# Combination, second gate and quantised feed-forward part in one block by batches, with the last weights quantised beside the first gate and the routing

## What is computed

```
x   = x + y0 * silu(layernorm(x))            # first gate, y0 from the first scan
xn  = layernorm(x); p, idx = top4(softmax(xn @ router))
x   = x + shared_expert(xn) + sum_k p[k] * expert[idx[k]](xn)   # the sum over k: "combination"
x   = x + y1 * silu(layernorm(x))            # second gate, y1 from the second scan
# last feed-forward part, weights in three values, activations in 8 bits, per token
ws  = mean(|W|) + eps;  Wq = clip(round(W / ws), -1, 1)      # for w_gate, w_up, w_down
xs  = 127 / max|xn|;    xq = min(round(xn * xs), 127)
h   = silu(xq @ Wq_gate / ..) * (xq @ Wq_up / ..)            # 2048 columns
hs  = 127 / max|h|;     hq = min(round(h * hs), 127)
out = x + (hq @ Wq_down) / ..
```

## Time and profile before

| | us |
|---|---|
| median of 3 runs (2230.44 to 2234.99) | 2232.67 |
| profiled execution, device time | 2233.23 |
| span of the profiled execution | 2231.4 |
| combine, second gate and last feed-forward part, of the span | 371.6 |

### The profile page before, as it was taken

How to read it: one execution, slowest core, us unless ns; L and a number is a source line. 1 busy time by engine, 2 the same in 40 slices (tenths; PEclk the granted TensorE clock), 3 DMA queues, 4 the chain that set the end, 5 groups by cost and what they waited for, 6 DMA issues and landing times. The chain is left out here.

```text
span 2231.4 us, 27149 instructions
## 1 busy us (share of the span) xinstructions
PE 1653.2 (74%) x8480; PEld 954.2 (43%) x8502; DVE 1758.9 (79%) x2275; ACT 1143.2 (51%) x1765; POOL 1337.3 (60%) x648
## 2 busy tenths in 40 slices
PE   5666757656538548999799998999989991005998
PEld 1222213222217435676466654666556660003554
DVE  3999999999965836998589867888578885856886
ACT  4675766766633014443444445555455550734776
POOL 0779788779953003888088844888368884652111
PEclk7888888989976569999999998999989996557999
DMA  6346546447552820000000432444424227650000
GB/s 218 117 162 202 183 154 231 145 158 248 179 196 76 160 68 11 10 10 15 33 11 1 149 135 97 157 166 156 161 102 156 86 72 289 190 159 2 23 25 29
DMA packets 127144, 264.63 MB, mean 119 GB/s; under 512 B 44546, under 2 KB 48386, under 8 KB 121794
## 3 DMA queue, kind: packets, MB, share of 16 engines
q1 hardware_dynamic: 93890, 184.24, 24.7%
q0 software_dynamic: 11520, 37.76, 5.8%
q10 hardware_dynamic: 21600, 40.90, 4.9%
HBM read 180.41 MB, written 82.44 MB: 118 GB/s over the span
## 5 line engine op out<-in xcount | busy, mean ns | idle before, releaser
L470 POOL TENSOR_TENSOR ssm_hs<-ssm_hs,ssm_Cs 128x1024 f32<-128x1024 f32 x128 | 314.7, 2458 | 146.5 <-DVE ssm_hs L433 142.5
L470 POOL TENSOR_TENSOR moe_hs<-moe_hs,moe_Cs 128x1024 f32<-128x1024 f32 x128 | 301.4, 2355 | 98.5 <-DVE moe_hs L433 97.5
L433 DVE TENSOR_TENSOR_SCAN moe_hs<-moe_dA,moe_bu 128x1024 f32<-128x1024 f32 x128 | 292.6, 2286 | 20.0 <-ACT moe_dA L347 10.1
L433 DVE TENSOR_TENSOR_SCAN ssm_hs<-ssm_dA,ssm_bu 128x1024 f32<-128x1024 f32 x128 | 292.7, 2287 | 17.3 <-ACT ssm_dA L347 0.5
L460 POOL TENSOR_TENSOR moe_U<-moe_U,moe_hs 128x1024 f32<-128x1024 f32 x128 | 302.0, 2360 | 6.0
L280 PE MATMUL ssm_pY<-ssm_hs,ssm_ident 128*128 128x512 f32 x512 | 276.9, 668 | 2.8 <-POOL ssm_hs L470 2.8
L1195 PE MATMUL moe_pgu<-moe_xsh,all_Wreg 128*128 128x256 f16 x1408 | 255.3, 279 | 12.8 <-DVE moe_hsl L1440 11.3
L1245 PE MATMUL moe_pgu<-all_Wreg,moe_xth 128*128 x1280 | 243.6, 313 | 0.0
L258 PE MATMUL ssm_pB<-ssm_bc,ssm_sel 96*128 96x512 bf16 x128 | 54.7, 427 | 204.9 <-DVE ssm_bu L424 204.6
L1195 PE MATMUL moe_pgu<-moe_xsl,all_Wreg 128*128 128x256 f16 x704 | 196.9, 280 | 0.0
L665 POOL TENSOR_TENSOR ssm_wlo<-ssm_wst,ssm_whi 128x1360 f16<-128x1360 f32 x64 | 186.5, 2914 | 0.0
(11 more groups left out here) (238 smaller groups left out, 3457.7 us busy)
## 6 DMA issues: line engine op xcount, KB each, us to landing
ssm_wst<-in_w_all SPq DMA_DIRECT2D x64, 680.0 KB, 4.9
w_hi<-ssm_whi SPq DMA_DIRECT2D x64, 340.0 KB, 2.3
w_lo<-ssm_wlo SPq DMA_DIRECT2D x64, 340.0 KB, 3.1
y_d<-moe_yo ACTq DMA_DIRECT2D x80, 256.0 KB
all_Wreg<-w_hi SPq DMA_DIRECT2D x16, 1088.0 KB
all_Wreg<-w_lo SPq DMA_DIRECT2D x16, 1088.0 KB
ssm_Cs<-c_d SPq DMA_DIRECT2D x64, 256.0 KB, 5.6
gate_Y<-y_ssm ACTq DMA_DIRECT2D x8, 1024.0 KB, 9.2
```

The lines of the kernel that those rows point to most:

```text
L433: self.nc.vector.tensor_tensor_scan(self.hs[:, j, :, :].rearrange("p k t -> p (k t)"), self.dA[:, q, :, :].rearrange("p k t -> p (k t)"), ...
L470: self.nc.gpsimd.tensor_tensor(self.hs[:, j, :, :], self.hs[:, j, :, :], self.Cs[:, i:i + 1, :].to_broadcast([P, HC, L]), ALU.mult)\
```

## The change

There are two parts.

**Ternary.** A new class holds the quantisation of the weights. In `gate(nc, 0, ...)` the eight pieces of w_gate and w_up are loaded by ACT's queue, and quantised matrix by matrix: ACT takes the absolute sums with an activation (`act_abs`) that DVE took, DVE and PE make the total and the scale, ACT does `up` (`act_up`), **POOL clips** (`pool_clip`, a tensor_scalar of 128x2048 in place, which DVE did), ACT does `out` and issues a store to DRAM. In `routing` the four pieces of w_down go the same way; DVE's total stands at g = 4 and its scale at g = 8 of the 64 steps. The last stage loads the three bfloat16 matrices (2 MB each) again.

**tail.** `combine`, `gate(nc, 1, ...)` and `quant_ffn` become one function with one block. Combination and second gate run ahead of the feed-forward loop by batches: nine tiles (AHEAD) are combined before the loop and one in each of the first seven steps; the four tiles of the next batch are gated after fixed parts of the loop (GATED), with y's transpose going through one PSUM buffer (`py`); the gate activations of the batch after the next are made by ACT in every fourth step, and Y and G have room for two batches. There are 16 gather buffers in place of 8.

```diff
 def gate(nc, l, d, X, y_ssm, r):
...
             def _(act):
...
+                if l == 0:
+                    for j in range(8):
+                        Q.act_load(act, j // 4, j % 4)
...
                     def evac(b):            # per tile c, behind the copy L803
+                        if b == 0:
+                            Q.act_up(act, 0, c)
+                        if b == 1:
+                            Q.act_out(act, 0, c)
+                            Q.act_abs(act, 1, c)
+                            Q.store(act, 0, c)
+                        if b == 2:
+                            Q.act_up(act, 1, c)
+                        if b == 3:
+                            Q.act_out(act, 1, c)
+                            if c:
+                                Q.store(act, 1, c - 1)
...
+                    Q.act_abs(act, 0, 0)
+                    Q.act_abs(act, 0, 1)
                     second(0)
+                    Q.act_abs(act, 0, 2)
                     second(1)
+                    Q.act_abs(act, 0, 3)
...
+                    Q.store(act, 1, 3)
+                    Q.stored(act)
...
             def _(pool):                    # behind the 16 products L820
+                for j in range(8 if l == 0 else 0):
+                    Q.pool_clip(pool, j // 4, j % 4)
...
 # DVE behind layernorm(b), PE ahead of router(b), for b in (0, 2)
+                            Q.dve_total(dve, b // 2)
+                            Q.dve_scale(dve, b // 2)
+                            Q.pe_total(pe, b // 2, ones[:])
...
 def routing(nc, d, r):
...
+                for k in range(4):          # ACT: 4 abs, 4 up, 4 x (out, store)
+                    Q.act_abs(act, 0, k)
...
+            def _(pool):
+                for k in range(4):
+                    Q.pool_clip(pool, 0, k)
...
+    def pool_clip(self, pool, z, k):
+        w = self.W[:, z, k, :]
+        pool.wait_ge(self.up_rdy, 4 * z + k + 1)
+        self.nc.gpsimd.tensor_scalar(w, w, ROUND + 1.0, ROUND - 1.0, ALU.min, ALU.max).then_inc(self.clip_rdy, 1)
...
+def tail(nc, d, r, X, y_ssm, out):          # POOL
+                for i in range(KC + 2):
+                    fetch(i)
+                for i in range(KC):
+                    y_gate(i)
+                fetch(KC + 2)
+                fetch(KC + 3)
+                x_clip(0)
+                for i in range(KC, 2 * KC):
+                    y_gate(i)
+                fetch(2 * KC)
+                for i in range(TT):
+                    if i + AHEAD < TT:
+                        fetch(i + AHEAD)
+                    if i + 1 < TT:
+                        x_clip(i + 1)
+                    b, t = divmod(i, KC)
+                    if t == KC - 1 and b + 2 < B:
+                        for j in range(KC):
+                            y_gate((b + 2) * KC + j)
...
+                for i in range(KC):         # DVE, ahead of its loop
+                    combine(i)
+                norm(0, 0, c_sd, c_rs, c_ln)
+                combine(KC)
+                combine(KC + 1)
+                for i in range(KC):
+                    gated(i)
+                norm(1, 0, a_sd, a_rs, a_ln)
                 x_scale(0)
+                combine(KC + 2)
                 x_scale(1)
+                combine(KC + 3)
+                norm(0, 1, c_sd, c_rs, c_ln)
+                combine(2 * KC)
                 for i in range(TT):
...
+                        if b + 1 < B and (t, f) in GATED:
+                            gated((b + 1) * KC + GATED[t, f])
...
+                    if i + AHEAD < TT:
+                        combine(i + AHEAD)
                     if i:
                         add(i - 1)
...
-        combine(nc, d, r, X, Wq, wsc)
-        gate(nc, 1, d, X, y_ssm, r)
-        quant_ffn(nc, d, r, X, Wq, wsc, out)
+        tail(nc, d, r, X, y_ssm, out)
```

More of the change, by code:

```diff
@@ L50 @@
 SHIFT = 2
+GATED = {(0, 3): 0, (1, 0): 1, (1, 2): 2, (1, 3): 3}
 def shared_pieces(c):
@@ L936, in _ @@
                 nc.scalar.activation(r["sig"][:], r["logit"][:, :, E], ACT.Sigmoid).then_inc(fin, 1)
+                for k in range(4):
+                    Q.act_abs(act, 0, k)
+                for k in range(4):
+                    Q.act_up(act, 0, k)
+                for k in range(4):
+                    Q.act_out(act, 0, k)
+                    Q.store(act, 0, k)
+                Q.stored(act)
+            @block.gpsimd
+            def _(pool):
+                for k in range(4):
+                    Q.pool_clip(pool, 0, k)
             @block.vector
@@ L1657, in quant_ffn @@
         pd = m.ps("pd", [P, H])
+        py = m.ps("py", [P, KC, P])
         loaded = m.sem("loaded")
+        w_in = [m.sem(f"w_in{i}") for i in range(3)]
+        y_in = [m.sem(f"y_in{i}") for i in range(B)]
+        got = [m.sem(f"got{i}") for i in range(NR)]
+        used = m.sem("used")
+        c_st = m.sem("c_st")
+        c_mv = m.sem("c_mv")
+        c_sd = m.sem("c_sd")
+        c_rs = m.sem("c_rs")
+        c_ln = m.sem("c_ln")
+        g_rdy = m.sem("g_rdy")
+        yg_rdy = m.sem("yg_rdy")
+        tr_rdy = m.sem("tr_rdy")
+        xa_rdy = m.sem("xa_rdy")
+        a_st = m.sem("a_st")
+        a_mv = m.sem("a_mv")
+        a_sd = m.sem("a_sd")
+        a_rs = m.sem("a_rs")
+        a_ln = m.sem("a_ln")
         eps_rdy = m.sem("eps_rdy")
-        sd_rdy = m.sem("sd_rdy")
-        ln_rdy = m.sem("ln_rdy")
         step = m.sem("step")
@@ L1692, in _, with fetch, y_gate, x_clip @@
                 sp.wait_ge(o_out, 16 * TT)
+            @block.gpsimd
+            def _(pool):
+                def fetch(i):
+                    for k in range(TOPK):
+                        g = i * TOPK + k
+                        if g >= NR:
+                            pool.wait_ge(used, g - NR + 1)
+                        nc.gpsimd.indirect_dma_start(
+                            out=yr[:, g % NR, :], out_offset=None, in_=r["y_d"],
+                            in_offset=bass.IndirectOffsetOnAxis(ap=r["pos"][:, i, k:k + 1], axis=0)).then_inc(got[g % NR], 16)
+                def y_gate(i):
+                    b, t = divmod(i, KC)
+                    if t == 0:
+                        pool.wait_ge(y_in[b], 16)
+                    pool.wait_ge(g_rdy, i + 1)
+                    y = Y[:, b % 2, t, :]
+                    nc.gpsimd.tensor_tensor(y, y, G[:, b % 2, t, :], ALU.mult).then_inc(yg_rdy, 1)
+                def x_clip(i):
+                    pool.wait_ge(xr_rdy, i + 1)
+                    if i >= 2:
+                        pool.wait_ge(tx_rdy, i - 1)
+                    nc.gpsimd.tensor_scalar(xq[:, i % 2, :], xn[:, i % 2, :], -ROUND, 127.0, ALU.add,
+                                            ALU.min).then_inc(xq_rdy, 1)
+                for i in range(KC + 2):
[13 more added lines that the diff above has]
+                        x_clip(i + 1)
+                    b, t = divmod(i, KC)
+                    if t == KC - 1 and b + 2 < B:
+                        for j in range(KC):
+                            y_gate((b + 2) * KC + j)
             @block.vector
@@ L1784, in _ @@
                 act.wait_ge(rnd_set, 1)
+                act.wait_ge(eps_rdy, 1)
+                root(0, 0, c_mv, c_sd)
+                for i in range(KC):
+                    gate_of(i)
+                root(1, 0, a_mv, a_sd)
                 layernorm(0)
@@ L1788, in _ @@
                 x_evac(0)
+                root(0, 1, c_mv, c_sd)
+                for i in range(KC, 2 * KC):
+                    gate_of(i)
                 for i in range(TT):
+                    b, t = divmod(i, KC)
                     for f in range(FC):
                         g = i * FC + f
+                        if f == 1 and t == 2 and b + 1 < B:
+                            root(1, b + 1, a_mv, a_sd)
+                        if f == 1 and t == 3 and b + 2 < B:
+                            root(0, b + 2, c_mv, c_sd)
                         act.wait_ge(gu_rdy, g + 1)
@@ L1802, in _ @@
                             layernorm(i + 2)
+                        if f >= 2 and t == 3 and b + 2 < B:
+                            for j in range(2):
+                                gate_of((b + 2) * KC + 2 * (f - 2) + j)
                     if i + 1 < TT:
@@ L1810, in _, with y_transpose @@
                     h_evac(TT - 1, a)
-            @block.gpsimd
-            def _(pool):
-                for i in range(TT):
-                    pool.wait_ge(xr_rdy, i + 1)
-                    if i >= 2:
-                        pool.wait_ge(tx_rdy, i - 1)
-                    nc.gpsimd.tensor_scalar(xq[:, i % 2, :], xn[:, i % 2, :], -ROUND, 127.0, ALU.add,
-                                            ALU.min).then_inc(xq_rdy, 1)
             @block.tensor
             def _(pe):
-                pe.wait_ge(loaded, 16)
+                pe.wait_ge(loaded, 32)
+                def y_transpose(i):
+                    b, t = divmod(i, KC)
+                    pe.wait_ge(yg_rdy, (b + 1) * KC)
+                    if i:
```

(9 more changed lines are left out.)

291 lines of the change are left out of this document (173 added, 118 removed).

## The result

The changed kernel takes 2244.62 us in the median of 6 runs (2239.85 to 2249.52), the kernel before, timed beside it, 2234.96 (6 runs). The ratio is 1.0042, with a 95% interval of 1.0028 to 1.0056: slower, by some 9.7 us, where 29 were forecast.

| stage | before | after | forecast for after minus before | measured |
|---|---|---|---|---|
| first scan | 654.0 | 653.3 | 0 | -0.7 |
| first gate | 73.9 | 100.4 | +45.4 | +26.5 |
| routing | 61.9 | 74.4 | +29.5 | +12.5 |
| experts and second scan | 1070.0 | 1074.7 | 0 | +4.7 |
| combination, second gate, feed-forward | 371.6 | 340.6 | -46.3 | -31.0 |

A forecast was written before the change was run, and what follows sets the result against it. No engine bounds the whole; each stage has its own limit: first gate a chain, routing DVE, final loop PE. 2233.23 + 45.4 (gate) + 29.5 (routing) - 46.3 (tail) = 2261.8, forecast 2262 us, range 2225 to 2288.

The forecast's parts named there:

- the rival with all idle time used: Tail loop: DVE's idle time takes the combination in, 15.2 us per tile, tail -64, total 2244 us; chance 0.15.
- the clip's price: Gate and routing: a POOL clip of 128x2048 taken as 6.6 us, between 6.2 and 7.7; lower bound 3.6.
- its rival: Gate and routing: POOL's float32 tensor_scalar is cheap, 3.6 us a clip, total 2231 us; chance 0.13.
- three signs of being wrong: Clips under 4.2 us; DVE TENSOR_SCALARs of 0.28 us beside a clip; a PE clock under 0.9 in the loop.
- The working for a cheap clip: First gate: with 3.6 us per clip the ACT work bounds instead, about +27 us.
- The lock: Gate and routing: DVE gets one SBUF-to-SBUF TENSOR_SCALAR through per POOL clip; in routing four clips are added whole, 26.4 us.
- The loads: Routing: four w_down loads share the DMA with the expert weights and put the first inputs back by about 2 us.
- Total and scale: Routing: these quantisation steps cost DVE 0.7 us.
- Before the loop 81.5: Tail: tile 8's gathers landed and combined 81.5 us behind the start, 98.9 us earlier than 180.4.
- "some 3" for Wq and y: Tail before the loop: transfer of the quantised weights and y beside gathers and products, some 3 us within 42.
- 17.7 per tile: Tail loop, tiles 0 to 6: 11.5 + 4.1 + 1.5 + 0.2 and 0.5 for x_clip's blocking; 43 us added.
- the clock rival: Early tail loop: half of PE's products at the lower clock add 3.4 us per tile, total 2286 us; chance 0.13.

The follow-up runs named there:

- the dear clip's run: Changed kernel with POOL's clip made of add 0 and min in place of min and max (lower bound left out); 2286.35 us in one run.
- the mended kernel: Changed kernel with gate copies first, w_up sums on DVE, w_down loaded later, routing clips on DVE, earlier tile-8 gathers, staged loads, spread additions; 2197.98 us.

## Why the prediction was wrong

Its direction was right and its size three times too large, and errors of opposite sign partly cancelled: gate and routing were forecast 35.9 us too dear (74.9 against 39.0), the tail 15.3 us too cheap. That the time lies near the 2244 of the rival with all idle time used is luck: that rival has tiles of 15.2 us, and they take 19.1.

**The step that failed is the clip's price.** "I take 6.6, between 6.2 and 7.7": it is 1.90. Even the lower bound, 3.6, was wrong, and so was its reason ("a POOL tensor_scalar is no cheaper at 512"): that scaled L1818, whose pair is add and min, to a clip whose pair is min and max. The prediction had noted the difference of the operation in its rival and then argued against it from a row on the output's width. Between clips of 1.9 and of 7.1 us (the dear clip's run) lie 17.4 us of the gate and 20.6 us of the routing; so this one number, 6.6 in place of 1.9, is worth more than the whole error, 2262 less 2244.62. Two of the three signs of being wrong that it named came, clips under 4.2 us and a clock under 0.9 in the loop.

**The gate.** The working for a cheap clip, about +27 with "the ACT work bounds instead", gave the right number, +26.5. The clips are hidden, and the run without the quantisation shows that the rest of it is the cause. How the 26.5 us divide is open: ACT's 45 us more of sums, ups and outs stand between PE's batches, but taking 14.6 of them out gave 2.3 us (sums on DVE), and taking w_up's out of the mended kernel 14.4. The prediction called the gate a chain in which no engine is full; from 692.6 on PE had been busy 32.4 of 35.3 us before the change, and its products now run more at the lower level, which makes 8.8 us more of busy time. No run takes that share out by itself. The first evacuation, forecast 39.4 us behind the stage's start, came at 38.2.

**The routing.** The lock was right in kind: during a clip DVE's step waits for its end, with a clip of 1.9 us and with one of 7.1. Its size is the clip less one step, 6.4 us for four, as a step passes between clips. The loads were "about 2 us" and measured 5.5: 4 MB ahead of seven small tables in the DMA. Total and scale took 0.3, and the stage's end behind the last step 0.3 more. Sum 12.5. (The prediction's own terms, 2, 0.7 and 26.4, add up to 29.1 and not to 29.5.)

**The tail.** -46.3 was forecast and -31.0 measured. Before the loop 81.5 against 87.8: the difference is DMA, "some 3" for Wq and y, and the run with staged loads has 81.1. In the loop 17.7 per tile (its terms add up to 17.8) against 19.1: 11.5, 4.3, 1.5 and 0.2 are there, and DVE's waits came along as said, but the rest is PE at half pace behind its idle time (1.7 us per tile in the rows above). So the clock rival, at 3.4 per tile, was half true. That these slower products lie on the path is read from the trace; no run took the clock away by itself. Tiles 0 to 6 are 9.5 us longer than forecast. Tiles 7 to 11 took 66.3 where 65.2 were forecast, the last four and the end were as before. (For a lost clock the prediction has -24 in one place and -22 in another.)

Two of the pages of the Trainium skill cited ahead, read against the runs. "GPSIMD Engine Reference", Performance versus the Vector engine, gave an estimate of 4.4 us for the clip, by a figure that the page has measured on a two-input operation; measured 1.90, less than half. The same section says that a body of up to two operations is bound by its port, 1.03 cycles per element: an estimate from that figure for 2048 columns at 1.2 GHz is 1.76 us. The clip's 1.89 agrees, while the 1.92 us at 512 columns of add and min do not. "SBUF — State Buffer", SBUF, says that the shared pair is locked for the whole instruction and the other engine blocks: the 7.07 us in the run with the dear clip agree. The page adds that DVE's `tensor_scalar` can take the pair in its faster mode; no run here tells that mode from another cause.

## What to carry to other kernels

Price an operation by a row of the same operation, its pair of operators included, not of the same instruction name; if there is none, that price is the widest bound of the sum and the range has to carry it. Work moved into a stage where an engine looks idle is paid where that stage is a chain of short steps: ask what each moved instruction stands in front of in its own queue (here ACT's copies, SP's tables, PE's router). And when a long piece of a hidden stage is put into a loop, cut it to the loop's own waits: the same additions cost 20 us less in four places, with their gathers a tile earlier, than in one.

## What the runs showed of the hardware

- A POOL tensor_scalar of 128x512 takes 0.61 to 0.62 us with min and max or mult and add, 1.50 with one operator, 1.92 with the other pairs tried; bfloat16 or float32 output makes no difference (0.61 and 0.61, 1.92 and 1.92). One operator alone is dearer than the fast pairs of two.
- DVE's TENSOR_SCALARs between SBUF buffers wait for the end of a one-input POOL instruction too: 1.88 us beside clips of 1.9, 7.07 beside clips of 7.1, 0.31 alone.
- DVE's BATCH_NORM_STATS2 did not wait for a clip: 2.46 us for four, most of them beside a clip of 7.1 us.
- After 4.2 to 5.7 us without work in the loop (tiles 1 to 4) PE ran its next eight products at 1.7 to 1.9 us for four, with a granted clock of 0.50 to 0.52, then at 1.03 and 1.00. In the run with spread additions the products behind a wait of 1.83 us ran at the higher level and those behind one of 2.06 us at the lower.
- The same expert stage took 1070.0 to 1077.9 us from run to run; differences of a few microseconds in a stage that no edit touches are no finding.
